# Two attentions of a fused decoder: a key spill placed ahead of the stacking, and weight pieces requested by another engine

## The reference, cut to what matters

```python
x = x + _L0_xattn_ref(_layernorm(x), ctx_1024, ctx_1024, W_q, b_q, W_k, b_k, W_v, b_v, W_o, b_o, mask)
...
qh = (q @ W_q.T + b_q).reshape(Bq, Sq, H, d_k).transpose(0, 2, 1, 3)   # 16 batches, 112 rows, 16 heads of 16
kh = (k @ W_k.T + b_k).reshape(Bq, Sk, H, d_k).transpose(0, 2, 1, 3)   # 375 keys
scores = jnp.einsum('bhqd,bhkd->bhqk', qh, kh) / math.sqrt(d_k)
attn = jax.nn.softmax(jnp.where(mask == 0, -inf, scores), axis=-1)
context = jnp.einsum('bhqk,bhkd->bhqd', attn, vh)
...
return context @ W_o.T + b_o
```

## Time and profile before

| | |
|---|---|
| median of 3 runs | 2326.16 us (2322.23 to 2326.8) |
| the profiled execution | 2323.39 us, span of its trace 2321.6 us |
| mean granted TensorE clock | 0.969 of full |
| PE busy | 2169.4 us, 93% of the span |
| DVE, ACT, POOL busy | 55%, 46%, 19% |
| attention 0 | from 0 to about 352 us |
| attention 3 | from about 1880 to 2235 us |
| DMA share, attention 0 / attention 3 / between | 0.70 / 0.68 / 0.21 |

### The profile page before, as it was taken

How to read it: one execution, slowest core, us unless ns; L and a number is a source line. 1 busy time by engine, 2 the same in 40 slices (tenths; PEclk the granted TensorE clock), 3 DMA queues, 4 the chain that set the end, 5 groups by cost and what they waited for, 6 DMA issues and landing times.

```text
span 2321.6 us, 46633 instructions
## 1 busy us (share of the span) xinstructions
PE 2169.4 (93%) x16038; PEld 1759.9 (76%) x16038; DVE 1285.7 (55%) x3563; ACT 1074.0 (46%) x2929; POOL 448.3 (19%) x478
## 2 busy tenths in 40 slices
PE   7999989999988899999999999999959979988998
PEld 6888877777666667678888788888747758877888
DVE  6877873222244522556556556555542238778766
ACT  5878872222223122244444444444402237877863
POOL 3112201111153345100000000000014421121150
PEclk9999999999999799999999999999969989999999
DMA  8677746222265322110000000001232257767701
GB/s 211 184 193 181 183 116 276 79 86 91 71 178 166 128 66 68 41 46 8 19 27 16 12 14 13 12 8 48 95 113 62 64 143 185 188 175 178 179 19 33
DMA packets 154867, 230.65 MB, mean 99 GB/s; under 512 B 66608, under 2 KB 127488, under 8 KB 152336
## 3 DMA queue, kind: packets, MB, share of 16 engines
q1 hardware_dynamic: 142160, 196.07, 30.4%
q0 software_dynamic: 10656, 29.37, 4.1%
q10 hardware_dynamic: 1824, 2.23, 0.4%
HBM read 176.36 MB, written 51.25 MB: 98 GB/s over the span
## 4 chain that ended last, share of the span: by engine, by line
PE 77%; DVE 7%; DMA 5%; issue 4%; SPq 3%; ACT 2%; POOL 1%; ACTq 0%; DVEq 0%; POOLq 0%
PE bank L2012 9%; PE bank L1157 8%; PE bank L2045 6%; PE bank L1188 6%; PE bank L1043 6%; PE bank L1039 6%; PE bank L2077 5%; PE bank L1083 4%; PE bank L1142 4%; PE bank L1028 3%; PE bank L1135 3%; PE bank L2062 3%; SPq L1523 2%; DMA query_halves<-arena 2%; PE bank L2398 2%
## 5 line engine op out<-in xcount | busy, mean ns | idle before, releaser
L1157 PE MATMUL bank<-ident,arena 112*125 112x112 f32 x2352 | 376.0, 278 | 2.2 <-DVE arena L1395 0.3
L1157 PEld LDWEIGHTS bank<-ident,arena 112*125 112x125 f32 x2352 | 342.8, 191 | 32.2 <-ACT arena L1428 5.8
L1428 ACT ACTIVATE arena<-arena,mx 112x375 f32<-112x375 f32 x512 | 309.3, 605 | 108.6 <-DVE mx L1374 104.5
L1374 DVE CUSTOM_DVE_ANT_0 arena<-bank,maskf 112x375 f32<-112x375 f32 x512 | 272.8, 541 | 101.3 <-PE bank L1135 96.8
L1428 ACT ACTIVATE arena<-bank,mx 112x375 f32<-112x375 f32 x272 | 154.8, 573 | 183.0 <-DVE mx L1386 155.4
L2012 PE MATMUL bank<-arena 128*128 x532 | 231.7, 558 | 2.1 <-ACT arena L2138 2.1
L1135 PE MATMUL bank<-kS,qS 128*112 128x376 f32 x512 | 204.9, 401 | 28.6 <-DMA qS<-query_halves 13.9
L1395 DVE COPY arena<-bank 125x336 f32<-125x336 f32 x448 | 214.1, 501 | 17.3 <-PE bank L1157 17.3
L1188 PE MATMUL bank<-arena 125*32 125x112 f32 (+1 forms) x4608 | 202.6, 265 | 3.1 <-DVE arena L1395 2.9
L1188 PEld LDWEIGHTS bank<-arena 125*32 125x32 f32 (+1 forms) x4608 | 144.3, 118 | 49.8 <-issue 32.5
L1435 ACT ACTIVATE arena<-bank 125x336 f32<-125x336 f32 x336 | 148.3, 442 | 45.4 <-PE bank L1157 44.4
(11 more groups left out here) (266 smaller groups left out, 3699.2 us busy)
## 6 DMA issues: line engine op xcount, KB each, us to landing
kS<-key_halves SPq DMA_DIRECT2D x256, 188.0 KB, 3.9
key_halves<-arena SPq DMA_DIRECT2D x64, 376.0 KB, 4.9
arena<-in_ctxT SPq DMA_DIRECT2D x62, 376.0 KB, 4.9
arena<-in_f_out SPq DMA_DIRECT2D x21, 768.0 KB, 4.5
qS<-query_halves SPq DMA_DIRECT2D x252, 56.0 KB, 2.2
arena<-in_f_up SPq DMA_DIRECT2D x4, 2816.0 KB, 20.0
arena<-results SPq DMA_DIRECT2D x38, 224.0 KB, 5.6
query_halves<-arena SPq DMA_DIRECT2D x32, 224.0 KB, 5.3
```

Of the source, the lines that this page charges most:

```text
L1157: m = pe.transpose(bank[2 + g % 2][0:KT, k * S:(k + 1) * S], pr[:, g % t.NR, k * KT:(k + 1) * KT], ident[0:S, 0:S])
L1374: dve.tensor_tensor_reduce(sm[:, g % 2, :], bank[g % 2][0:S, 0:SK], maskf[:, :], -t.a["scale"], 3e38, ALU.add, ALU.min, mx[:, g % t.NR:g % ...
L1428: act.activation(pr[:, g % t.NR, :], src, ACT.Exp, bias=mx[:, g % t.NR:g % t.NR + 1], scale=-1.0, accum_out=row_sum(t, b)[:, h:h + 1]).the ...
```

## The change

For batches 2 to 15 of both attentions the spill of key tile 1 moves from behind the stacks of queries and key tile 0 to the place ahead of all stacks. Batches 0 and 1 have programs of their own, which are not touched. The 8 pieces of the shared weights leave SP's program: POOL requests them, each when PE has made the values of its batch; its place in POOL's order is slot 15 of the window of batch b. In attention 3 the first piece takes the second bias of the block along (128 KB), as before.

```diff
@@ steps
             if self.stack:
+                for b in range(2, 2 + SHARED_PIECES):
+                    extras[(b - 1) * H + 15].append(("load", b))
                 extras[1].append(("half", "k", 1))
@@ stack_sync, batch(b)
                 spill_keys(0)
                 if b >= 2:
                     sp.wait_ge(t.scores, t.h0 + (b - 1) * t.H)
+                spill_keys(1)
                 stack_queries()
                 stack_keys(0)
-                spill_keys(1)
                 stack_keys(1)
@@ stack_sync
                     sp.wait_ge(t.gen_ready, values_done(t, b))
                     context(sp, t, b + 2)
-                if 2 <= b < 2 + SHARED_PIECES:
-                    late(b - 2)
@@
+        def load_in(pool, t, b):
+
+            pool.wait_ge(t.gen_ready, values_done(t, b))
+            if t.L == 0:
+                shared_piece(pool, part(ffn[0].at["shared"], ffn[0].size), A["f0_shared"][0], b - 2, ffn[0].w_shared)
+            else:
+                shared_sync(pool, ffn[3], b - 2)
+
         def att_gpsimd(pool, t):
             for s in t.plan:
-                if s[0] == "half":
+                if s[0] == "load":
+                    load_in(pool, t, s[1])
+                elif s[0] == "half":
```

More of the change, by code:

```diff
@@ L1525, in queries_stacked, with stack_sync @@
                         .then_inc(t.stacked[b % 2], 16)
-        def stack_sync(sp, t, late):
+        def stack_sync(sp, t):
             def batch(b):
@@ L2553, in _ @@
             weight_0(sp, 0, "q")
-            stack_sync(sp, att[0], lambda n: shared_piece(sp, part(ffn[0].at["shared"], ffn[0].size),
-                                                              A["f0_shared"][0], n, ffn[0].w_shared))
+            stack_sync(sp, att[0])
             sp.wait_ge(stage_done, 3 * 1)
@@ L2595, in _ @@
             sp.wait_ge(stage_done, 3 * 6)
-            stack_sync(sp, att[3], lambda n: shared_sync(sp, ffn[3], n))
+            stack_sync(sp, att[3])
             sp.wait_ge(stage_done, 3 * 7)
```

## The result

The changed kernel takes 2367.05 us (median of 4 runs, 2362.93 to 2370.73), against 2324.19 for the kernel before on the same chip: ratio 1.0188, 95% interval 1.0159 to 1.0217. The forecast was 2340, in a range of 2328 to 2354. The sign is right and the size is not: +43 us instead of +14. The profiled execution took 2368.71 us.

A forecast was written before the change was run, and what follows sets the result against it. PE was taken as the bound, waiting 14.7 us for stacked keys. Attention 0's +9.5 and attention 3's +4.1 made 13.6, with something for batches 2 and 3 +14: 2337 from the profiled run, 2340 us against the median; range 2328 to 2354.

The forecast's parts named there:

- All 12 DMAs that head 0 needs are queued behind that wait, and PE waits for them: SP's queue: query and key tile 0 stacks follow SP's wait for DVE's lower half of tile 1; head 0 waits 1.1 to 1.4 us.
- These times hang on PE's order, which doesn't change: DVE's lower half of tile 1 ends at fixed times, in attention 0 T+9.63 in odd and T+10.58 in even windows.
- offsets: Times from T to SP's first query stack, forecast at T+10.1 in odd windows and T+11.1 in even ones.
- T: Start of head 0 of the former batch on PE, from which the times within a batch's window are counted.
- X: Time from SP's first query stack to the landing of key tile 0's last stack, taken as 10.2 us.
- Attention 3, +4.1: Its 14 windows from batch 2 on, 286.1 us before, were to take 290.2.
- The pieces leave SP: 0: SP issues one DMA of about 0.45 us less in 16 batches, where it would be waiting for products: no gain.
- the pieces come to POOL: 0: POOL is busy less than a fifth of the time; delay put at 0 to 0.3 us a batch, 0 in the sum.
- The rival with the pieces taking turns: Pieces on POOL's queue share DMA engines with the stacks, 8 x 1.2 us; part of the slower rival, chance 0.18.
- slower by more: Pieces delay the stacks, or repeated waits of PE let the clock fall once or twice: 2350 to 2355 us, chance 0.18.
- The faster rival, 0.08: SP's loop is the true bound and the stacks land within 9 us, so PE's waits go: 2307 us, chance 0.08.
- What would show it: Signs listed for traces: first query stack times, head 0 waits, weight loads waiting some 30 us, key spill waits under 20.

The follow-up runs named there:

- e3: Kernel before, with only the wait for DVE's lower half of key tile 1 added ahead of the query stacks, spill unmoved: 2352.82 us, 1.0137.
- e5: Changed kernel, with DVE's lower half of key tile 1 one slot earlier in DVE's order: 2328.91 us, 1.0017.
- e6: Changed kernel, with POOL's context split placed four heads later in its list, which left POOL's order and waits the same: 2365.42 us, 1.0175.
- e7: Changed kernel, with 8 needless score products by PE ahead of its wait for the stacks, batches 2 to 14: 2359.57 us, 1.0144.
- e11: Changed kernel, with 6 needless products ahead of PE's wait and POOL's context split held until 8 heads are made: 2352.20 us, 1.0120.
- e9: Changed kernel, with POOL's split of even batches' contexts held until PE has made 8 heads of the window: 2362.14 us, 1.0168.
- e1: Kernel before, with only the spill of key tile 1 moved ahead of all stacks, pieces left on SP: 2360.47 us, 1.0160.
- e2: Changed kernel, with the spill of key tile 1 put back, so only the pieces move to POOL's queue: 2316.93 us, 0.9982.
- e4: Kernel before, with key tile 1's spill between the query stacks and key tile 0's stacks, pieces on SP: 2305.14 us, 0.9923.

## Why the forecast was right in sign and wrong in size

By the prediction's steps:

- **"All 12 DMAs that head 0 needs are queued behind that wait, and PE waits for them": right**, and shown by e3, where nothing but the wait is added (+30 us), and by e5, where nothing but its end is moved (the loss nearly gone).
- **"These times hang on PE's order, which doesn't change": the step that failed.** PE's order didn't change, its speed did. Tile 1's lower half comes at a fixed distance from T only at one clock. After a fall it comes up to 3.1 us later, the stacks with it, and the window is longer by as much. The 14 offsets of attention 0 add up to 164.1 instead of 148.5: +15.6, of which some 2.9 are DVE's stretched scalings and the rest, 12 to 13, low clock. In the trace the clock stands at the lower level for 30.7 us of these windows, where it did for 6.8 before. These sizes are of one trace: in e6's, of the same program, the offsets are 10.3 over the forecast's. By the medians, fillers that keep the clock up bring 7.5 us (e7) and 9.9 (e11 against e9).
- **X = 10.2: too small by 0.3.** It came out at 10.5 in attention 0, +4.3 over 14 windows. A 376 KB spill "which must be carried by the same DMA engines" had been given 0.1 at most, 10.2 against batch 2's 10.1. With it ahead of the stacks X is 10.4 to 10.7 in attention 0 (the change, e1, e6, e7, e9, e11), with the same wait and no spill ahead 10.1 (e3). But in e5 the spill is ahead as well, and X is 10.2, so that the spill as the reason is not shown. With 15.6 the 4.3 are the whole miss in attention 0, 20.0.
- **Attention 3, +4.1: came out at +11.5.** Offsets 152.2 in place of 146.7 (+5.5), X 10.25 (+0.7), and 1.2 from rounding and from three even windows in which PE's own work, and not the stacks, comes last by 0.3 to 0.6. 6.8 us are at low clock, 3.4 before.
- **"The pieces leave SP: 0", "the pieces come to POOL: 0".** Alone they bring 5.6 us (e2). Behind the moved spill nothing of it can be seen: with e1 and the change on different chips, 1.0160 and 1.0188, intervals overlapping, no gain or loss of theirs can be told. The rival with the pieces taking turns isn't borne out.
- **The rival "slower by more", 2350 to 2355, chance 0.18: its clock half was the case, far underpriced.** I counted "one or two falls" of 3 us, from one long wait of 3.4 and because "waits of 1.4 left no such mark". Most waits of the changed kernel lie between the two, and there were six stretches of low clock in attention 0 and two in attention 3. It is the count that was wrong, and not the price of one. The three long stretches (6.8 us) moved the first query stack by 2.8 to 3.1 us, the three short ones (3.4 us) by 1.5 to 1.6, which is about the full clock lost in them. The forecast also had the place wrong: it counted falls apart from the offset, while a fall moves the offset itself, and so the wait at the window's end doesn't absorb it. Nor does that wait grow: in attention 0 it is 1.33 us on average at the end of the six windows with a fall and 1.77 at the end of the eight without, and none of the six was followed by another fall (in e6 one of five was).
- **The faster rival, 0.08:** right that SP's loop cost PE time before (e4: -17 us), wrong that this order would give it back.
- **What would show it:** first query stacks at T+10.1 and T+11.1 in windows without a fall or overlap, as foreseen; head 0 waits in all 14 windows of attention 0 and in ten of attention 3; weight loads wait 40 us, where some 30 was said; SP's key spill waits under 20: 4.5; the context load in batch 9 at T+19.3.

Shown by runs: the wait as cause (e3), the moment of the lower half as what sets its size (e5), the low clock as an amplifier worth some 10 us (e11 against e9), the best of the orders tried (e4). Open: why the windows of attention 3 are longer than forecast with the clock held up, why X is larger, most of the 4.3 us outside the 28 windows, and the exact split of the 15.6, since a fall and a stretched scaling can meet in one window and two executions of one program differ by 5.5 us there.

## What to carry to other kernels

An issuing queue that works in order should hold its waits where it is busy until they are over anyway, not ahead of what the bounding engine waits for: between the query and key stacks the same spill makes this kernel 0.8% faster, ahead of both 1.6% slower. When a forecast rests on "so many us after T", ask whether the engine that counts them keeps its clock, and how often it may lose it: a short wait added to every window can bring a fall in many of them, and a fall delays the result that the next wait is for, so that the wait doesn't make up for it. A fixed time from T that is about to become the bound is also the place to look for a gain: e5 shows that some 1.5 us of it are worth 38.

## What the runs showed of the hardware that I had not expected

- **The clock falls after short waits, in work that is otherwise dense.** In attention 0 of the changed kernel it went to the lower level at 62.6, 127.4, 175.2, 219.6, 287.9 and 328.8 us, for 3.4 or 6.8 us each time. Head 0 had just waited 1.86, 1.83, 1.67, 1.67, 1.67 and 2.53 us. After waits of 0.5 to 1.1 it never fell; after others of 1.7, 1.8, 1.85 and 2.36 it didn't either, nor after one of 2.28 in e9, so the wait's length alone doesn't decide. What else does is not settled by these runs. That these waits have a part in it is shown by the fillers below, which put work into them and leave the rest of the program as it is.
- **A few needless products in the wait held it at the full level.** With 8 of about 0.17 us each there was no fall in the 14 windows of attention 0 (e7); with 6 there was one (e11), and without any three in the run that differs from it by the fillers alone (e9).
- **A DVE instruction can last as long as POOL's.** The scaling of 0.35 us took 1.65 where POOL's 128x752 TENSOR_TENSOR (1.78) ran, and ended within 0.15 us of it; with POOL's kept away it was 0.35 again. The Trainium skill (Advanced Engine Details and Errata, VectorE Performance Modes) notes that DVE's second port to SBUF is shared with GpSimd, and that GpSimd's instructions and DVE's in a two-port mode can block each other. The rows agree with such a block, and put 1.3 us on it here; whether this scaling ran in a two-port mode they don't show.
